# Layer 1 of a fused two-layer kernel: three convolution lags placed before the rotary softmax, squares on ScalarE and a halved last store at the end

## The reference

```python
x = x + _L1_attn_ref(_L1_cond_ref(x, cond, ...), gamma, Wq, Wkv, Wo)      # causal attention with rotary positions
x = x + _L1_ffn_ref(_L1_cond2_ref(x, cond), w_fc, w_proj)

def _L1_cond2_ref(x, w):    # depthwise causal convolution over time, one filter of K = 64 taps per channel
    ...                     # taps = cond: K = 64, of which only 32 lags reach into a sequence of 32 tokens
def _L1_ffn_ref(x, w_fc, w_proj):
    h = jnp.maximum(turbo_linear(x, w_fc), 0.0)     # 256 -> 1024
    return turbo_linear(h * h, w_proj)              # 1024 -> 256
```

## Time and profile before

| | before |
|---|---|
| median of 3 runs | 1491.93 us (1489.49 to 1497.31) |
| profiled execution, its own time | 1491.9 us |
| its span in the profile | 1490.1 us |
| PE busy | 1349.9 us, 91% |
| DVE busy | 1119.1 us, 75% |
| ACT busy | 824.9 us, 55% |
| POOL busy | 146.7 us, 10% |
| granted TensorE clock, mean | 0.975 |

### The profile page before, as it was taken

How to read it: one execution, slowest core, us unless ns; L and a number is a source line. 1 busy time by engine, 2 the same in 40 slices (tenths; PEclk the granted TensorE clock), 3 DMA queues, 4 the chain that set the end, 5 groups by cost and what they waited for, 6 DMA issues and landing times.

```text
span 1490.1 us, 23006 instructions
## 1 busy us (share of the span) xinstructions
PE 1349.9 (91%) x7954; PEld 969.8 (65%) x7954; DVE 1119.1 (75%) x2862; ACT 824.9 (55%) x1694; POOL 146.7 (10%) x167
## 2 busy tenths in 40 slices
PE   6988888899999999999999967898999999999996
PEld 2433333578777777777877745475767777777765
DVE  4999999858857575757575979768687787878674
ACT  3866766875566666767676673534443434434221
POOL 0000000101010101010101100010210102020101
PEclk9999999989999999999999989798999999999999
DMA  9322333520111010101012310000000000000000
GB/s 379 97 64 64 71 84 81 153 79 29 36 36 43 29 43 29 43 29 43 29 44 82 149 64 8 22 15 1 15 12 10 14 7 21 7 8 8 8 8 15
DMA packets 26364, 73.78 MB, mean 50 GB/s; under 512 B 3977, under 2 KB 4885, under 8 KB 24993
## 3 DMA queue, kind: packets, MB, share of 16 engines
q1 hardware_dynamic: 25696, 71.62, 15.4%
q10 hardware_dynamic: 576, 0.98, 0.2%
HBM read 49.52 MB, written 23.07 MB: 49 GB/s over the span
## 4 chain that ended last, share of the span: by engine, by line
PE 52%; DVE 34%; ACT 7%; issue 5%; DMA 1%; SPq 1%; POOL 0%; DVEq 0%; ACTq 0%; POOLq 0%
PE psum L600 11%; PE psum L931 7%; PE psum L707 7%; DVE h_all L1820 5%; DVE work L1820 4%; PE psum L646 4%; PE psum L633 4%; DVE ffn_mem L1941 3%; PE psum L970 3%; DVE work L1952 3%; PE psum L960 2%; PE psum L613 2%; PE psum L877 2%; DVE work L1948 1%; ACT probs_t L1288 1%
## 5 line engine op out<-in xcount | busy, mean ns | idle before, releaser
L600 PE MATMUL psum<-h_all,w_big 128*128 128x256 f32 x1024 | 246.9, 389 | 3.9 <-ACT work L1246 3.9
L600 PEld LDWEIGHTS psum<-h_all,w_big 128*128 128x128 f32 x1024 | 190.3, 193 | 42.7 <-issue 13.5
L1820 DVE SCALAR_TENSOR_TENSOR work<-work,taps 128x248 f32<-128x248 f32 (+30 forms) x558 | 151.5, 346 | 0.0
L554 PE MATMUL psum<-w_big,h_all 128*64 128x512 f32 x512 | 124.1, 606 | 0.0
L931 PE MATMUL psum<-work,w_big 128*128 128x256 f32 x512 | 116.4, 380 | 0.0
L1820 DVE SCALAR_TENSOR_TENSOR h_all<-h_all,taps 128x248 f32<-128x248 f32 (+30 forms) x434 | 116.0, 342 | 0.0
L707 PE MATMUL psum<-w_big,gru_mem 128*128 128x256 f32 x512 | 113.6, 379 | 0.5 <-ACT gru_mem L1300 0.5
L707 PEld LDWEIGHTS psum<-w_big,gru_mem 128*128 128x128 f32 x512 | 96.4, 190 | 13.8 <-ACT gru_mem L1300 0.6
L931 PEld LDWEIGHTS psum<-work,w_big 128*128 128x128 f32 x512 | 95.5, 190 | 14.8 <-issue 2.5
L960 PE MATMUL psum<-w_big 128*128 128x256 f32 x448 | 105.0, 387 | 0.0
L1277 ACT ACTIVATE work<-psum 32x128 f32<-32x128 f32 x256 | 68.3, 267 | 53.7 <-PE psum L633 51.2
(11 more groups left out here) (316 smaller groups left out, 2628.1 us busy)
## 6 DMA issues: line engine op xcount, KB each, us to landing
value_rows<-w_emb SPq DMA_DIRECT2D x128, 128.0 KB, 2.3
work<-value_rows SPq DMA_DIRECT2D x16, 1024.0 KB, 5.8
w_big<-in_Wq SPq DMA_DIRECT2D x2, 2048.0 KB, 17.3
w_big<-in_Wo SPq DMA_DIRECT2D x2, 2048.0 KB, 21.8
out<-w_big SPq DMA_DIRECT2D x16, 256.0 KB, 2.0
x_res<-out SPq DMA_DIRECT2D x15, 256.0 KB, 2.7
w_big<-in_Wv SPq DMA_DIRECT2D x1, 2048.0 KB, 18.3
w_big<-in_Wk SPq DMA_DIRECT2D x1, 2048.0 KB, 23.8
```

Source lines behind the costliest of these rows:

```text
L554: mm = pe.matmul(bank(4 + n)[j * B:(j + 1) * B, :], h_all[:, k, :, 2 * pair + j], w_big[:, 2, k * H * HD + n * 512:k * H * HD + (n + 1) * ...
L600: mm = pe.matmul(bank(n % 2)[:, o * TA:(o + 1) * TA], w_big[:, s, k * H * HD + at:k * H * HD + at + HD], h_all[:, k, bass.ds(i * BA, BA), ...
L1820: ins = dve.scalar_tensor_tensor(dst[:, :, lag:], src[:, :, :T - lag], tap, dst[:, :, lag:], ALU.mult, ALU.add)
```

## The change

1. DVE, calls 1 to 7: `conv2(range(4, 7))` stands right after the last head's products, ahead of `rot_soft_in`. Where it stood, three lags are left (7 to 9) in calls with `cond`.
2. DVE, call 7: the remaining lags of chunk 6 (7 to 31) go ahead of the late add of chunk 5.
3. ACT, call 7: `keep_x3(7)` goes ahead of the first two ReLUs of chunk 6.
4. ACT and POOL, chunks 6 and 7: the squares are done by ACT, each right after its ReLU, and no longer by POOL.
5. PE, DVE, SP, chunk 7: each half of `pj(7)` goes to a bank of its own and raises the semaphore by itself; each half is added (128x256) and stored (128 KB) by itself.

```diff
+        def pj_out(c, g):
+            return bank(6 + g)[:, 0:D] if isinstance(c, int) and c == NA - 1 else bank(6)[:, g * D:(g + 1) * D]
+        def own_squares(c):
+            return isinstance(c, int) and c >= NA - 2
...
+                if c < NA - 1:
+                    store(c)
+            for g in range(GA):
+                sp.wait_ge(y_on.sem, NA + g)
+                sp.dma_start(out[:, GA * (NA - 1) + g:GA * (NA - 1) + g + 1, :], y_buf[:, g:g + 1, :]).then_inc(y_out, 16)
+            sp.wait_ge(y_out, (NA + 2) * 16)
...
                     for f in range(KF):
-                        mm = pe.matmul(bank(6)[:, g * D:(g + 1) * D], h2_t[:, f, g * P:(g + 1) * P], proj_t[:, f, :],
+                        mm = pe.matmul(pj_out(c, g), h2_t[:, f, g * P:(g + 1) * P], proj_t[:, f, :],
                                        start=(f == 0), stop=(f == KF - 1))
+                    if isinstance(c, int) and c == NA - 1:
+                        mm.then_inc(pj_sum.sem, 1)
...
                     act.activation(relu[:, f % 2, :], bank(f % 2)[:, 0:TA], ACT.Relu).then_inc(relu_on.sem, 1)
+                    if own_squares(c):
+                        act.wait_ge(relu_on.sem, KF * c + f + 1)
+                        act.activation(h2_t[:, f, :], relu[:, f % 2, :], ACT.Square).then_inc(h2_on.sem, 1)
...
+                if rot and not cond:
+                    keep_x3(i)
                 if ffn:
                     relus(ni, range(0, 2))
                 if prep:
                     row_squares(i + 2)
-                if rot and not cond:
-                    keep_x3(i)
...
-                for f in tiles:
+                for f in (() if own_squares(c) else tiles):
                     pool.wait_ge(relu_on.sem, KF * c + f + 1)
...
                 turn_heads(H)
+                conv2(range(4, 7))
                 if rot:
                     rot_soft_in(i, 0, rlink)
...
+                if rot and not cond:
+                    conv2(range(7, T))
                 if late:
                     dve.wait_ge(res_on.sem, ni)
                     dve.wait_ge(pj_sum.sem, ni)
...
-                conv2(range(4, 10))
+                if cond:
+                    conv2(range(7, 10))
                 if cond:
                     cond_soft_out(ci, 1, clink)
-                conv2(range(10, T))
+                if cond:
+                    conv2(range(10, T))
...
+                    if rot:
+                        dve.wait_ge(pj_sum.sem, ni + 1)
+                        dve.tensor_tensor(y_buf.rearrange("p g n -> p (g n)"), bank(6),
+                                          ffn1(ni)[0].rearrange("p g n -> p (g n)"), ALU.add).then_inc(y_on.sem, 1)
+                    else:
+                        for g in range(GA):
+                            dve.wait_ge(pj_sum.sem, ni + g + 1)
+                            dve.tensor_tensor(y_buf[:, g, :], pj_out(ni, g), ffn1(ni)[0][:, g, :],
+                                              ALU.add).then_inc(y_on.sem, 1)
```

More of the change, by code:

```diff
@@ L516, in _ @@
                     load_r(c + 2)
-                store(c)
-            sp.wait_ge(y_out, (NA + 1) * 16)
+                if c < NA - 1:
[4 more added lines that the diff above has]
+            sp.wait_ge(y_out, (NA + 2) * 16)
         @block.tensor
@@ L994, in pj @@
                     for f in range(KF):
-                        mm = pe.matmul(bank(6)[:, g * D:(g + 1) * D], h2_t[:, f, g * P:(g + 1) * P], proj_t[:, f, :],
+                        mm = pe.matmul(pj_out(c, g), h2_t[:, f, g * P:(g + 1) * P], proj_t[:, f, :],
                                        start=(f == 0), stop=(f == KF - 1))
-                if GA - 1 in groups:
+                    if isinstance(c, int) and c == NA - 1:
+                        mm.then_inc(pj_sum.sem, 1)
+                if GA - 1 in groups and not (isinstance(c, int) and c == NA - 1):
                     mm.then_inc(pj_sum.sem, 1)
@@ L2464, in chunk1 @@
                     dve.wait_ge(y_out, 16 * ni + 16)
-                    dve.wait_ge(pj_sum.sem, ni + 1)
-                    dve.tensor_tensor(y_buf.rearrange("p g n -> p (g n)"), bank(6),
-                                      ffn1(ni)[0].rearrange("p g n -> p (g n)"), ALU.add).then_inc(y_on.sem, 1)
+                    if rot:
[7 more added lines that the diff above has]
+                                              ALU.add).then_inc(y_on.sem, 1)
                 if rot and cond:
```

## The result

| | before | changed |
|---|---|---|
| median | 1491.93 us (7 runs, 1489.49 to 1497.31) | 1481.33 us (7 runs, 1480.35 to 1481.86) |
| profiled execution, its own time | 1491.9 us | 1480.35 us |
| its span | 1490.1 us | 1478.6 us |
| granted clock, mean | 0.975 | 0.978 |

The ratio is 0.9922 with a 95% interval of 0.9909 to 0.9935. Between the medians that is 10.6 us, by the ratio 11.6 (9.7 to 13.6), where 5.7 had been forecast. The direction was right; the forecast had about half of the size.

A forecast was written before the change was run, and what follows sets the result against it. Each trip was taken as bound by DVE from the scores to fc, by PE from fc to the next scores. Savings 2.75 + 0 + 2.02 + 0.35 + 0.29 + 0.30 = 5.71 us from 1491.9 gave 1486.2 us, range 1481.5 to 1490.0.

The forecast's parts named there:

- part 4: Squares on ACT: chunk 6 costed at nothing, as nobody waits; chunk 7's last square saves 0.35 us (0.2 to 0.45).
- part 1: Three lags before the rotary softmax: 0.55 us in each of calls 2 to 6, nothing in call 1, 2.75 us.
- A: Rival: the exponential does not bind, DVE takes all 2.13 us in calls 2 to 6; 1477.8 us; 5%.
- C: Rival: moved lags overrun the wait for the scores in all seven calls; loses if d exceeds 0.82 us; 3%.
- Rival B: TensorE's clock before fc: falls go away, 1483.9 us (at most 1482.3), 20%; or all five fall, 1489.7, 15%.
- Part 2: Call 7, lags ahead of the late add: second add still waits for PE's projection, 0 us (0 to 0.1).
- Part 3: Call 7, keep_x3 first: ACT's copy lets DVE go at 1447.90, so the last convolution starts 2.02 us earlier.
- Part 5: Chunk 7's halves at the end: last add 0.29 us shorter, halved store 0.3 us shorter.

## Why the prediction was right and wrong

Of the 4.9 us by which the forecast fell short, two terms that its sum held at nothing make up the whole: POOL's squares beside the last convolution (part 4, 2.2 us) and the falls of TensorE's clock (part 1, 2.8 us).

**Part 1, the queues: right to 0.01 us.** The transpose still waits 0.22 us (0.29 of room was left), the reduction waits 1.48 for ACT (about 1.5), PE's idle time is 2.25, the trip is 68.38 to 68.39, call 1 gives nothing. The two runs with the exponential first show that the wait is for that exponential and no other. A falls, since the exponential did bind; so does C, since the lags fit ahead of the scores.

**Part 1, the clock: a failed step, seen and given the wrong weight.** Rival B asked whether the falls would go away at 2.25 us and gave that 20%, against 15% for the other side, because with one trace the falls came without a visible rule. They became rarer (14 of 25, then 5 of 30; in calls 3 to 6 12 of 20, then none of 24). And the forecast took the profiled execution's two falls as the usual state; five profiles with the same gap have 2.8 of them at 4.2 us. The term should have been some 2.8 to 3.6 us in the sum, not in a rival. The row that said so was there: no fall after 0.51 us of idle time, two in five after 2.8. The rule that was cited there from the Trainium skill (TensorE: Matmul & The Clock Gate, The HAM clock gate), that activity releases the throttle, agrees with the direct test with four matmuls (3.4 us less). That less idle time can only help, as was drawn from it there, does not hold call by call: call 2 fell more often at 2.25 us than at 2.8.

**Part 2, 0 us: right.** The lags end at 1434.3, the second add waits 4.84 us for PE's projection.

**Part 3, 2.0 us: right in the timetable, but not by itself.** Alone it gave some 1.25 in the timetable, since it moved the convolution further under POOL's squares.

**Part 4: the other failed step.** "Nobody waits for chunk 6" is true of the results of the squares, and I costed their move at nothing by it. It is not true of what POOL's work does to DVE beside it: 2.2 us for the last convolution with the copy in its old place, 3.0 with the copy first. The trace of before would have shown it, had the lags been read in time slices. The 62 lags of falling width took 18.59 us there, and the 56 of the convolution before it, without POOL beside them, 14.10. In the first 5 us of the 62, with POOL at work, eight started, half of them 0.80 us or longer; in the first 4.3 us of the 56, 13 started, of 0.39 to 0.45 us. For chunk 7's last square 0.24 came instead of 0.35: PE stood idle for 1.01 us before pj(7), where 0.9 had been forecast.

**Part 5, 0.59: 0.56 measured.** The half add takes 0.42, the half store lands in 1.7 us after 2.0. The rule that was cited for it from the Trainium skill (DMA: Bandwidth & Descriptors, Anatomy of one DMA) is given there for DMAs issued from GpSimd, and this store is issued by SyncE: its difference of 0.3 us agrees, its level of 2.6 and 2.3 us is above both measured ones.

**Sum.** 2.75 + 2.8 (clock) + 1.99 + 2.2 + 0.24 + 0.56 = 10.5 us, or 11.3 with 3.6 for the clock, beside 10.6 between the medians and 11.6 by the ratio; the runs do not tell the two apart. What is not settled is fc(7): 9.38 and 8.86 in the two profiles, 7.17 in two others with the same 2.6 us of idle PE before it as the changed kernel. Nor does a run tell why, at the same idle time, some calls have falls and others none.

## What to carry to other kernels

When an engine's work is moved off, ask not only who waits for its result, but who reads beside it: a two-input product on POOL nearly doubled the time of two-input instructions on DVE. When an instruction is moved out of a bound stretch, follow the queue to the next cross-engine wait: it took 1.58 of 2.13 us, and reordering that other engine's queue gave them back. And look at how long TensorE idles in each trip of a loop: half a microsecond less, or a few matmuls for nothing, was worth as much as the moved work itself.

## What the runs showed of the hardware

- A scalar_tensor_tensor of 128 x 224 to 248 on DVE took 0.44 us alone and 0.82 (medians) beside POOL's product of two 128x256 tiles; beside a fill on POOL it was not slowed. POOL itself took 0.61 to 0.84 for the product.
- POOL's multiplication of one tile by a constant took 0.91 to 1.12 us beside the lags, longer than its product of two tiles of the same size.
- In the work that followed 2.8 us without a matmul the granted clock fell to 1.2 GHz in 14 of 25 cases, judged by its length, after 2.25 us in 5 of 30, after 1.06 us or less in none of 15. A fall cost 1.15 to 2.5 us. Where the windows show it, it began 0.2 to 1.3 us after the matmuls had begun again, not in the idle time.
